# Inverse roots of the normalisations as a power on GpSimd, in a two-layer perceiver block on one core

## The reference

```
def _layernorm(x, eps=1e-05):                  # ahead of each of six blocks
    return (x - mean(x)) / sqrt(var(x) + eps)

x = x + cross_attention_16_heads(_layernorm(x), ctx)
x = x + gated_convolution_mixer(_layernorm(x))   # begins with x * rsqrt(mean(x*x) + 1e-6) * w
x = x + quantised_ffn(_layernorm(x))             # layernorm, int8-like up, gelu, layernorm, down
x = x + cross_attention_1_head(_layernorm(x), ctx)
x = x + rotary_attention_16_heads(_layernorm(x))
x = x + mixture_of_8_experts(_layernorm(x))
```

## Time and profile before

| | us |
|---|---|
| median of 3 runs | 1020.67 |
| lowest, highest | 1020.07, 1023.71 |
| the profiled execution's own time | 1022.15 |
| its span | 1020.4 |
| TensorE busy | 922.4 |
| VectorE busy | 607.9 |
| ScalarE busy | 498.1 |
| GpSimd busy | 76.2 |

### The profile page before, as it was taken

One profiled execution on the slowest core, in us unless ns is written; L12 is line 12 of the kernel. 1 busy time (PEld: TensorE's weight loads), 2 busy tenths in 40 slices (PEclk: granted clock), 3 DMA queues, 4 the chain that ended last, 5 costly groups with the idle time before them and its releaser, 6 DMA issues.

```text
span 1020.4 us, 15374 instructions
## 1 busy us (share of the span) xinstructions
PE 922.4 (90%) x6046; PEld 550.5 (54%) x6046; DVE 607.9 (60%) x1121; ACT 498.1 (49%) x983; POOL 76.2 (7%) x86
## 2 busy tenths in 40 slices
PE   5469799999999999999988999598999989999878
PEld 2236444444555555555544677355866845466656
DVE  4647777777884448888823686857223136388240
ACT  1624366777775557777787333234213012677111
POOL 2312001111000000000000100101000016000000
PEclk9779899999999999999999799698999979999989
DMA  9835644445322112223432500727419050000000
GB/s 355 226 88 162 210 136 114 133 125 156 102 75 89 32 34 66 76 75 88 144 119 94 211 1 1 247 68 259 168 42 368 2 165 1 0 2 1 1 1 21
DMA packets 66374, 108.70 MB, mean 107 GB/s; under 512 B 6902, under 2 KB 40438, under 8 KB 64374
## 3 DMA queue, kind: packets, MB, share of 16 engines
q1 hardware_dynamic: 64092, 100.35, 31.2%
q10 hardware_dynamic: 2208, 7.34, 1.9%
HBM read 93.77 MB, written 13.89 MB: 106 GB/s over the span
## 4 chain that ended last, share of the span: by engine, by line
PE 79%; DVE 7%; ACT 6%; issue 3%; DMA 3%; SPq 1%; POOL 0%; ACTq 0%; DVEq 0%
PE psum L1752 12%; PE psum L1734 10%; PE psum L1705 10%; PE psum L2102 5%; PE psum L2073 5%; PE psum L1689 5%; PE psum L1873 5%; PE psum L1679 4%; PE psum L2165 4%; PE psum L1886 3%; PE psum L2197 3%; ACT arena L730 2%; DVE arena L1066 2%; PE psum L2211 2%; PE psum L2297 1%
## 5 line engine op out<-in xcount | busy, mean ns | idle before, releaser
L1066 DVE TENSOR_REDUCE arena<-psum 128x1 f32<-128x1024 f32 x256 | 301.8, 1219 | 122.9 <-PE psum L1705 122.8
L730 ACT ACTIVATE arena<-psum 128x512 f32<-128x512 f32 x512 | 264.9, 603 | 64.1 <-PE psum L1734 63.1
L1734 PE MATMUL psum<-arena 99*128 99x256 bf16 x1024 | 161.9, 276 | 8.4 <-ACT arena L730 4.8
L1705 PE MATMUL psum<-arena 96*128 96x512 bf16 x512 | 153.6, 384 | 6.9 <-DVE arena L1066 5.5
L1734 PEld LDWEIGHTS psum<-arena 99*128 99x128 bf16 x1024 | 80.5, 98 | 107.7 <-ACT arena L730 50.9
L1752 PE MATMUL psum<-arena 128*32 128x256 f32 x2048 | 136.8, 385 | 0.0
L1752 PEld LDWEIGHTS psum<-arena 128*32 128x32 f32 x2048 | 53.5, 109 | 75.4 <-ACT arena L730 36.9
L1679 PE MATMUL psum<-arena 128*128 128x512 f32 x128 | 66.0, 645 | 22.3 <-DMA arena<-wkT 9.2
L1689 PE MATMUL psum<-arena 128*128 128x256 f32 x256 | 62.9, 389 | 1.3 <-ACT arena L708 1.3
L1705 PEld LDWEIGHTS psum<-arena 96*128 96x128 bf16 x512 | 49.6, 99 | 26.6 <-DVE arena L1066 13.3
L1689 PEld LDWEIGHTS psum<-arena 128*128 128x128 f32 x256 | 48.0, 193 | 17.1 <-issue 10.1
(11 more groups left out here) (241 smaller groups left out, 984.7 us busy)
## 6 DMA issues: line engine op xcount, KB each, us to landing
arena<-kparts SPq DMA_DIRECT2D x192, 128.0 KB, 3.1
kparts<-arena SPq DMA_DIRECT2D x32, 384.0 KB, 3.3
arena<-ctxT SPq DMA_DIRECT2D x18, 512.0 KB, 5.2
arena<-ctx SPq DMA_DIRECT2D x2, 4096.0 KB, 14.4
arena<-mask SPq DMA_DIRECT2D x8, 1024.0 KB, 5.2
arena<-mask ACTq DMA_DIRECT2D x4, 1024.0 KB, 12.3
arena<-ctxT SPq DMA_DIRECT2D x1, 4096.0 KB, 12.9
arena<-ctxT SPq DMA_DIRECT2D x4, 1024.0 KB, 8.7
```

The costliest lines, as they stand in the source:

```text
L730: nc.scalar.activation(PR[step % 4][:, pair * CH:(pair + 1) * CH], ring_bank(slot), ACT.Exp)\
L1066: nc.vector.tensor_reduce(MX[g % 2][:, col:col + 1], unit_banks(n).rearrange("p b n -> p (b n)"), AX.X, ALU.max).then_inc(s_maxed, 1)
L1705: last = nc.tensor.matmul(out, q, KST[g % 2][0:ROWS, j, at], start=True, stop=not masked, skip_group_check=True)
L1734: last = nc.tensor.matmul(ring_heads(slot)[:, u, :], KST[gg % 2][0:KROWS, j, kc * P:(kc + 1) * P], QST[0:KROWS, G * g + j, b * S:(b + 1) * S],
```

## The change

The square roots on ScalarE and the reciprocals on VectorE go. In their place GpSimd raises the variance plus eps to the power -0.5, in place in SD[:, 4:8], with a tensor of exponents NHALF that a memset fills once. `ask_root` and the count `ln_var` stay as they are; GpSimd's `root` waits for them and counts up `ln_sd`, for which VectorE's `take_root` waits and then goes on at once. The eleven calls of `root` stand in GpSimd's queue in the order in which VectorE asks, between the work that it had. The function for the gain of the odd tile gets a name (`gain_odd`). ScalarE's first instruction on a table (a square root of a constant) goes as well.

```diff
+            nc.gpsimd.memset(NHALF, -0.5).then_inc(ln_sd_ready, 1)
+            def root(first=0, last=TT):
+                roots[0] += 1
+                pool.wait_ge(ln_sd_ready, 1)
+                pool.wait_ge(ln_var, roots[0])
+                part = SD[:, 4 + first:4 + last]
+                nc.gpsimd.tensor_tensor(part, part, NHALF[:, first:last], ALU.pow).then_inc(ln_sd, 1)
+
+            root()
             nc.gpsimd.memset(V[:, :, :, DH:VW], 1.0).then_inc(built, 1)
...
             pool.wait_ge(on["c_padded"], 2)
+            root()
+            root()
...
-            for b in range(B):
+            def gain_odd(b):
                 pool.wait_ge(on["d_centred"], b + 1)
                 odd = UH[2 * b + 1][:, 0, :]
                 nc.gpsimd.tensor_tensor(odd, odd, row("g2"), ALU.mult).then_inc(on["d_gained"], 1)
+            root(0, 2)
+            root(0, 2)
+            gain_odd(0)
+            root(2, 4)
+            root(0, 2)
+            root(2, 4)
+            gain_odd(1)
+            root(2, 4)
+            root()
...
             act.wait_ge(built, 3)
-            nc.scalar.activation(TABLES[:, 0:1], ONES[:, 0:1], ACT.Sqrt)
-            act.wait_ge(ln_var, 1)
-            nc.scalar.activation(SD[:, 0:4], SD[:, 4:8], ACT.Sqrt).then_inc(ln_sd, 1)
             load_ctx(3)
...
-            def root(first=0, last=TT):
-                sqrts[0] += 1
-                act.wait_ge(ln_var, sqrts[0])
-                nc.scalar.activation(SD[:, first:last], SD[:, 4 + first:4 + last], ACT.Sqrt).then_inc(ln_sd, 1)
...
             dve.wait_ge(ln_sd, 1)
-            nc.vector.reciprocal(SD[:, 4:8], SD[:, 0:4]).then_inc(ln_step, 1)
-            dve.wait_ge(ln_step, 2 * TT + 1)
...
-            def take_root(first=0, last=TT):
+            def take_root():
                 roots[0] += 1
                 dve.wait_ge(ln_sd, roots[0])
-                mark(nc.vector.reciprocal(SD[:, 4 + first:4 + last], SD[:, first:last]))
-                done()
```

More of the change, by code:

```diff
@@ L183, in build @@
         MSUM = f32(at, 8); at += 8
-        TABLES = f32(at, 2); at += 2
+        TABLES = f32(at, 1); at += 1
+        NHALF = f32(at, 4); at += 4
         FLAG = arena[0:1, at:at + 1].bitcast(I32); at += 1
@@ L371, in build @@
         ln_sd = sem("ln_sd")
+        ln_sd_ready = sem("ln_sd_ready")
         h_ready = sem("h_ready")
@@ L614, in _ @@
                                         pattern=[[-1, P]], channel_multiplier=1).then_inc(built, 1)
+            nc.gpsimd.memset(NHALF, -0.5).then_inc(ln_sd_ready, 1)
+            roots = [0]
+            def root(first=0, last=TT):
[5 more added lines that the diff above has]
+            root()
             nc.gpsimd.memset(V[:, :, :, DH:VW], 1.0).then_inc(built, 1)
@@ L758, in _ @@
                             sum_mask(part)
-            nc.scalar.activation(TABLES[:, 1:2], ONES[:, 0:1], ACT.Exp)
+            nc.scalar.activation(TABLES[:, 0:1], ONES[:, 0:1], ACT.Exp)
             copy_tops(0)
@@ L776, in _ @@
             copy_context(GROUPS - 1)
-            sqrts = [1]
-            def root(first=0, last=TT):
-                sqrts[0] += 1
-                act.wait_ge(ln_var, sqrts[0])
-                nc.scalar.activation(SD[:, first:last], SD[:, 4 + first:4 + last], ACT.Sqrt).then_inc(ln_sd, 1)
             turns = [1]
@@ L804, in _ @@
             copy_turned(HTC)
-            root()
-            root()
             copy_turned(HTC, "norm_w")
@@ L868, in _ @@
             copy_ha(1)
-            root(0, 2)
             copy_hb(1)
@@ L931, in _ @@
             copy_hidden(1)
-            root(2, 4)
-            root(0, 2)
             copy_turned_half(0)
@@ L1205, in deviation @@
                 ask_root(first, last, factor, eps)
-                take_root(first, last)
+                take_root()
             def aggregate(n, first=0, last=TT):
@@ L1393, in _ @@
             ask_root(0, 2, 1.0 + 1e-5, 1e-5 * 1e-5)
-            take_root(0, 2)
+            take_root()
             dve.wait_ge(on["rows_loaded"], 48)
@@ L1415, in _ @@
             ask_root(2, 4, 1.0 + 1e-5, 1e-5 * 1e-5)
-            take_root(2, 4)
+            take_root()
             add_down(0)
             ask_root(0, 2)
-            take_root(0, 2)
+            take_root()
             centre_for_keys(0)
```

## The result

| | us |
|---|---|
| changed kernel, median of 20 runs | 1026.13 |
| its lowest and highest | 1019.66, 1030.10 |
| kernel before, median of 20 runs beside it | 1022.18 |
| ratio, 95% interval | 1.0035 (1.0019 to 1.0050) |
| profiled execution of the changed kernel, its span | 1026.13, 1024.3 |

The changed kernel is slower by 0.35%, about 3.6 us (3.95 by the two medians of the table). Forecast were 2.2 us more, a ratio of 1.0022 that lies inside the interval, and "within 0.5%"; the 1022.9 us of the forecast stood on a median of 1020.67, which in the 20 runs here is 1022.18. The number came out near; the runs show that it did so for reasons that the prediction had only in part, since TensorE's clock takes a share that the prediction never mentions.

A forecast was written before the change was run, and what follows sets the result against it. TensorE, busy 922.4 of 1020.4 us, was taken as the bound, so only its waits counted. Terms +0.9, +0.5 and +0.8 gave +2.2 us on 1020.7, so 1022.9 us; 8-in-10 range 1018.5 to 1031.5.

The forecast's parts named there:

- within 0.5%: Whole kernel: change in time of less than about 5.1 us, which a measurement can't tell; chance 0.67.
- The power's duration, X = 0.6: Each GpSimd power lasts 0.6 us, the geometric middle of 0.327 and 1.201; range 0.1 to 3.4.
- The handover of 0.08 and 0.03: GpSimd starts 0.08 us after VectorE's asking; VectorE goes on 0.03 us after the power.
- Four open roots, +0.23 each: Norms at about 572, 659, 828 and 962 us, where TensorE waits: stretch 0.71 against 0.48 us, together +0.9.
- The gelu norm of batch 0, +0.5: At 641 us: power held until VectorE's bias additions L1342 end, by the shared SBUF port; +0.5 us, undisturbed -0.1.
- a root that starts inside the bias additions: At 641 us: named beforehand as a sign that the prediction was wrong.
- The gelu norm of batch 1, +0.8: At 694 us: reciprocal gone, so GpSimd's gain L651 starts ahead of VectorE's L1351; order turns, +0.8 us.
- Table loads at nothing: ScalarE: 13 of 17 table loads go, 16.7 us, but they are hidden; costed at nothing.
- Rival 2: ScalarE's time was worth something: loads removed at 710.89 and 871.74 give TensorE -2.6 us; 1017.9 us; chance 0.13.
- Roots with slack, transfers, the moved weight products: Remaining roots, ScalarE's DMAs behind the first root, and weight products moved from 560 to about 575 us: no cost.
- The sum: Whole kernel: +0.9 +0.5 +0.8 = +2.2 us, giving 1022.9 us.
- Rival 1: GpSimd's power is slow, from 1.2 us: five us per us of its duration; 1031.4 or 1043 us; chance 0.27.

The follow-up runs named there:

- double: Changed kernel with every power computed twice on GpSimd, first into a spare place; 1030.95 us, ratio 1.0093 to the kernel before.
- open_on_scalar: Changed kernel with the roots at mixer, cross-attention of batch 0, rotary attention and experts back on ScalarE and VectorE; 1021.77 us, ratio 1.0008 to the kernel before.
- product: Changed kernel with the power replaced by a product 1.0 x 1.0, handovers and queues kept; 1021.64 us, ratio 0.9997 to the kernel before.
- late_gain: Changed kernel with one useless VectorE reciprocal of 0.16 us behind the gelu root of batch 1; 1028.87 us in a single run.
- no_square_root: Kernel before with ScalarE's square roots written as copies, freeing it of 13 table loads; 1021.90 us, ratio 1.0012.
- wait_at_572: Kernel before with four useless reciprocals, 0.8 us, behind the mixer's first root at 572 us; 1025.35 us, ratio 1.0030.
- one_again: Second timing of the changed kernel with only the root at 659 us back on ScalarE and VectorE; 1029.69 us, ratio 1.0072 to the kernel before.
- one_on_scalar: First timing of the changed kernel with only the root at 659 us back on ScalarE and VectorE; 1029.51 us, ratio 1.0069 to the kernel before.

## Why the prediction was right, and where not

*The power's duration, X = 0.6.* Mis-sized. It is 1.01 us at four elements and 0.70 at two; I took the middle between a product and a large subtraction. The runs show that a power on GpSimd costs 0.157 us for each element and a product 0.002 ((0.250 - 0.189) / 31 from one element to 32), so no product of the rows was near it. The true values lay inside the bounds kept, 0.1 to 3.4.

*The handover of 0.08 and 0.03.* 0.17 (0.14 at 641) and 0.03. The 0.08 of the earlier trace rows was behind an instruction of 512 elements and a single wait; here it is a tiny instruction, and `root` has two waits, of which the trace shows one as an instruction of its own (L625, 11 times, 0.02 us, some 0.1 us ahead of the power). Which of these makes the start later, no run tells.

*Four open roots, +0.23 each.* The places were right, and TensorE's waits grew there alone. The sizes were 0.73, 0.40, 0.71 and 0.71, together 2.55 instead of 0.9; of the mixer's 0.73, TensorE was only 0.57 late at 601. double and open_on_scalar show that the loss hangs on them.

*The gelu norm of batch 0, +0.5.* The step failed: I had the power held up by the two-SBUF additions L1342, as the large pair in the earlier trace rows is. It wasn't. It started 0.24 us into them and took 0.74 instead of 0.70, and the additions took 0.76 instead of 0.75. The lateness at 648 is 0.14 more than at 601. The prediction had named a root that starts inside the bias additions as a sign that it was wrong. The Trainium skill, page "SBUF — State Buffer", section "Who interferes with whom", has a lock between such a pair; the row at 641 shows nothing of one between a tiny power and these additions, and by it the term would have been 0.5. At 699 the same rule agrees with the trace: VectorE's L1353 lasted 3.33 instead of 1.28 us behind GpSimd's gain. The product of two elements in the kernel product wasn't held up there either (0.24 us), so it isn't the power's slow arithmetic that spares it, and its small operands are what is left. Products of 16 elements were slowed beside VectorE's work, from 0.32 to 0.82 us.

*The gelu norm of batch 1, +0.8.* Right in mechanism and size: the order turned at 695 in every kernel without the reciprocal, for 0.90 to 0.92 us; late_gain turned it back with one instruction and lost nothing there.

*Table loads at nothing.* Right. 13 loads of 1.283 us less, and no_square_root stays within 0.31% of the kernel before. Rival 2 falls: its -2.6 us lie outside the interval, which reaches to -0.7. The Trainium skill's 2.66 us for a switch ("ScalarE: Activation LUTs", "What ACT_TABLE_LOAD costs") would not have changed this, and the loads here show 1283 ns and an idle time of 0.0 ahead of three of the four.

*Roots with slack, transfers, the moved weight products.* Nothing, as forecast, though the products didn't take 0.33 us but 0.60 beside VectorE; the cover was large enough.

*The sum.* The terms of the path as measured are 1.12 up to 660, 0.91 for the order, 0.71 and 0.71: 3.45 us. The prediction had 2.2. That the measured 3.6 is close to 3.45 is partly chance, and so is the nearness of the forecast: roots that cost 1.65 more than forecast, a term of 0.5 that came out at 0.14, and a loss and a gain by the clock nearly cancelled. The step that is missing from the prediction is the clock: it had TensorE's matmuls cost the same wherever they come. In the changed kernel the clock takes 2.4 at 660 to 669 and gives about 2.0 back before 832. In wait_at_572 a path term of 0.58 becomes 3.4 in the profile and 3.0 by the ratio (1.0030), and in one_again, with a path of 3.0, the time is 7.0. So a term that I take off the path need not come off the time: three open roots back on ScalarE (2.15 us of the path) bring 1.4 us by the ratios, which overlap, one (0.40) makes it 3.9 us worse, all four (2.55) bring 2.8.

*Rival 1* (X from 1.2) did not come about, but X = 1.01 was nearer to it than to the forecast, and its price of five us per us of X is borne out in kind: one more power at each root, 1.0 or 0.7 us (4.4 us over the four open roots and the one at 641), cost 5.9 us.

*What stays open.* What decides whether the clock comes back at 662, and how much it gives back at 812 to 832, I can't say. Two delays 90 us apart each went with a low clock, 0.15 us of lateness didn't and 0.40 did, and 6.56 us in double didn't again. In how many executions of one kernel the clock stays low there isn't known, since each kernel but two (the changed one and the one with one root back) has one profile. Why one_again gets back only 0.5 us up to 832 and loses 1.9 more up to 965, where one_on_scalar (2.3) and double (1.9) do the like and the others lose at most 1.1, wasn't tried; so why this kernel is slower than the changed one stays unexplained. Executions of one kernel spread over up to 12 us (7.8 and 10.4 in the twenty runs of the two kernels), so a profile's account holds for that execution.

No version beat the kernel before beyond its measurement: the best form that computes the result, open_on_scalar, is even with it.

## What to carry to other kernels

Ask of a function on another engine what it costs per element before asking what it frees: 16.7 us freed on an engine with slack were worth nothing, and 0.4 to 0.7 us more at each of four places where TensorE waits started the loss. Where TensorE idles at its lower clock and then starts again, a delay of a few tenths ahead of that point can cost several times itself (0.40 became 3.33 us in a profile, 1.6 by the ratio of the times), and a longer one may not; look at the granted clock of the stretch behind each wait that an edit lengthens, and give it a wider range than the sum of the path. And compare a kernel's lateness at fixed places of TensorE's work, not only its end: the end hides a loss and its return.

## What the runs showed of the hardware

- A power (tensor_tensor, fp32) on GpSimd takes 0.559, 0.709, 1.007, 1.637, 2.899 and 5.426 us for 1 to 32 elements in each partition; a product of 32 takes 0.250.
- 16-element products with a scalar on GpSimd take 324 to 327 ns beside an idle VectorE and 817 beside its convolutions (604 in the mean of all 16); a two-element power (0.74 against 0.70) and a two-element product (0.24 against 0.19) nearly keep their durations beside a VectorE addition with two SBUF inputs.
- The same eight fp32 matmuls 128x128x256 take 1.99 us with the clock up and 3.78 at the lower level; in one profile each, 0.40 us more of waiting ahead of them, or 0.6 us of delay carried in from 90 us earlier, went with the lower level for both groups, while in double, with a wait of 3.77 us, they took 3.71 and 1.99.
- A handover from VectorE to GpSimd took 0.14 to 0.17 us behind a tiny instruction, and back 0.03.
